# A decoder layer on one core: constants loaded in five groups, their splits placed in the engines' orders, and two semaphores for the pair moves

## The reference

```
kv_c = rms_norm(x @ W_kv) * g_kv ; q_c = x @ W_q                      # latents, 64 and 128 wide
k = [kv_c @ W_kdec | rope(x @ W_krope)] ; q = [q_c @ W_qdec | rope(q_c @ W_qrope)]
x = layernorm(x + softmax(causal(q k^T / sqrt(48))) (kv_c @ W_vdec) @ W_o)   # 16 heads
x = layernorm(x + softmax(x ctx^T / 4) ctx @ W^T + b)                         # 16 heads of 16
x = layernorm(x + sum over the top 2 of 8 experts of w_e * (gelu(x @ W1_e + b1_e) @ W2_e + b2_e))
```

## Time and profile before

| what | time |
|---|---|
| median of three runs | 777.57 us (777.42 to 779.69) |
| the profiled execution | 772.65 us |
| its span, from first to last instruction | 770.8 us |
| TensorE busy in the span | 630.1 us (82%) |
| mean granted clock of TensorE | 0.932 of 2.4 GHz |

### The profile page before, as it was taken

The page is one execution under the profiler, slowest core; times in us unless marked ns, Lnnn a source line. Parts: engine busy times, 40 slices in busy tenths (PEclk is TensorE's granted clock), DMA queues, the critical chain, the costliest instruction groups (busy, mean ns, idle before and its releaser), DMA issues.

```text
span 770.8 us, 22764 instructions
## 1 busy us (share of the span) xinstructions
PE 630.1 (82%) x8056; PEld 453.7 (59%) x8057; DVE 519.7 (67%) x1113; ACT 380.2 (49%) x791; POOL 320.6 (42%) x276
## 2 busy tenths in 40 slices
...
GB/s 237 58 148 124 206 63 119 40 104 26 98 70 14 112 42 73 69 26 114 71 97 137 56 82 74 64 28 43 41 41 44 52 41 41 48 47 41 43 32 213
DMA packets 39799, 59.34 MB, mean 77 GB/s; under 512 B 6736, under 2 KB 27472, under 8 KB 39600
## 3 DMA queue, kind: packets, MB, share of 16 engines
...
...
## 4 chain that ended last, share of the span: by engine, by line
PE 44%; DVE 11%; ACT 4%; DMA 3%; issue 3%; POOL 1%; ACTq 0%; DVEq 0%; POOLq 0%
PE bank L1562 7%; PE bank L1184 4%; PE bank L1564 4%; DVE mxc L946 3%; PE bank L1210 3%; PE bank L1552 3%; ACT probs L702 2%; PE max_scores L1552 2%; PE bank L1554 2%; DMA x_sb<-x_rows,slot_row 2%; PE max_scores L1554 2%; PE max_scores L1553 2%; PE bank L1553 2%; PE exp_scores L1538 2%; PE exp_scores L1249 2%
## 5 line engine op out<-in xcount | busy, mean ns | idle before, releaser
L702 ACT ACTIVATE probs<-exp_scores 128x768 f32<-128x768 f32 (+1 forms) x128 | 117.5, 918 | 111.7 <-PE exp_scores L1241 50.4
L606 POOL DMA_INDIRECT acc_rows<-x_res,slot_row x39 | 65.3, 1674 | 122.1 <-DVE x_res L1102 119.1
L1562 PE MATMUL bank<-w_sb,wp 128*128 x312 | 110.0, 380 | 2.0 <-DVE wp L1089 2.0
L946 DVE TENSOR_REDUCE mxc<-max_scores 128x4 f32<-128x1024 f32 x64 | 78.1, 1221 | 31.6 <-PE max_scores L1255 31.3
L1564 PE MATMUL bank<-w_sb,wp 128*128 x312 | 85.1, 273 | 0.0
L911 DVE TENSOR_REDUCE mx<-max_scores 128x6 f32<-128x768 f32 x64 | 60.9, 952 | 25.6 <-PE max_scores L1223 25.6
L1087 DVE CAST wp<-probs 128x512 f16<-128x512 f32 x78 | 33.6, 431 | 64.5 <-ACT probs L765 64.5
L765 ACT ACTIVATE probs<-bank,b_sb 128x128 f32<-128x128 f32 x152 | 43.5, 370 | 65.2 <-PE bank L1554 65.2
L765 ACT ACTIVATE probs<-max_scores,b_sb 128x128 f32<-128x128 f32 x160 | 45.6, 369 | 59.6 <-PE max_scores L1554 59.6
L1184 PE MATMUL bank<-probs,w_sb 128*32 128x256 f32 x768 | 58.6, 410 | 6.8 <-ACT probs L702 6.0
L1552 PE MATMUL max_scores<-xT,w_sb 128*128 128x128 f16 x320 | 60.5, 222 | 1.2 <-DVE xT L1081 1.2
...
## 6 DMA issues: line engine op xcount, KB each, us to landing
w_sb<-w_sb SPq DMA_DIRECT2D x192, 64.0 KB, 2.1
wstage<-in_w_exp SPq DMA_DIRECT2D x16, 512.0 KB, 4.0
w_sb<-in_w_exp SPq DMA_DIRECT2D x8, 512.0 KB, 4.0
wp<-in_w_exp SPq DMA_DIRECT2D x8, 512.0 KB, 4.2
...
```

Source lines behind the costliest of these rows:

```text
L606: nc.gpsimd.indirect_dma_start(out=acc_rows[:, :], out_offset=bass.IndirectOffsetOnAxis(ap=slot_row[:, n:n + 1], axis=0), in_=yb[n % 2], i ...
L702: nc.scalar.activation(probs[:, 2 * (k % 2):2 * (k % 2) + 2, 0:cols], ps_e[:, :, 0:cols], ACT.Exp, scale=(SELF_SCALE, CROSS_SCALE)[a]).the ...
L946: nc.vector.tensor_reduce(mxc[:, 2 * k:2 * k + 2, :], ps_m[:, :, :].rearrange("p h (a k) -> p h a k", a=2), axis=AX.X, op=ALU.max).then_in ...
L1562: mm(o[:, 0:2 * D], ah[:, u, f, :], weights(e, at, 2 * D), start=(f == 0), stop=(f == FC - 1), skip_group_check=True)
```

## The change

It does five things.

- The constants are five groups (`rl0` to `rl4`), each with a semaphore of its own, and are units of SyncE's order: `rl0` = w_kv and w_q, `rl1` = the rotated weights, `rl2` = the content weights and the values' weight, `rl3` = g_kv and the table, `rl4` = masks, wo, xb, wx, wg, bg, b1, followed by the stores of zero rows, for which SyncE no longer waits (`z_st`; ScalarE waits for it ahead of the first `sv`, GpSimd ahead of the gathers).
- The splits of projection weights are units: `ph0` to `ph2` on ScalarE, `pl0` to `pl2` on VectorE; the six copies of identity and masks are `mk`. TensorE waits at the first unit that needs each one.
- The raw weights lie elsewhere in the buffer, in an order that fits the groups.
- The moves of content raise `c_mv[k]`, the moves of rotated rows `r_mv[k]`, so casts and copies wait only for the moves that read what they overwrite.
- `cb` and `cw` use PSUM bank 3 and `cn` uses bank 0, where all three used bank 1. All five tables are new.

```diff
+    "rl": "load_constants", "ph": "projections_high", "pl": "projections_low", "mk": "masks",
 TENSOR_ORDER = """
-la.0 kt.0 qk0.0 qk1.0 qk2.0 qk3.0 va.0 la.1 ct0.0 ct1.0 kt.1 qk0.1 qk1.1 sm0.0 qk2.1 qk3.1 sm1.0 sm2.0 sm3.0 ct0.1
+la.0 kt.0 qk0.0 qk1.0 qk2.0 qk3.0 va.0 ct0.0 la.1 ct1.0 kt.1 qk0.1 sm0.0 ct0.1 qk1.1 sm1.0 qk2.1 sm2.0 qk3.1 sm3.0
...
 SYNC_ORDER = """
-x.0 w0.0 w1.0 c.0 w2.0 x.1 x.2 mc0.0 mc1.0 mc2.0 mv0.0 w3.0 mv1.0 x.3 mc3.0 mv2.0 mc4.0 mv3.0 mc5.0 mc6.0 w0.1 mv4.0
+w0.0 rl0.0 rl1.0 x.0 w1.0 rl2.0 rl3.0 x.1 w2.0 rl4.0 c.0 x.2 mv0.0 mv1.0 mc0.0 mc1.0 mc2.0 mc3.0 mv2.0 mc4.0 mc5.0
...
-        ps_max = [ps_x[i] for i in (2, 1)]
+        ps_max = [ps_x[i] for i in (2, 0)]
...
-        ps_back = [ps_x[i] for i in (0, 1)]
-        ps_out = [ps_x[i] for i in (0, 1)]
+        ps_back = [ps_x[i] for i in (0, 3)]
+        ps_out = [ps_x[i] for i in (0, 3)]
...
+                elif u == "load_constants":
+                    for dst, src in const_loads[k]:
+                        sp.dma_start(dst, src).then_inc((r_ld + [t_ld, c_ld])[k], 16)
+                    if k == 4:
+                        sp.wait_ge(c_ms, 1)
+                        sp.dma_start(x2_rows[TOK:ROWS, :], oP[0][:, 0, :]).then_inc(z_st, 16)
+                        sp.dma_start(acc_rows[TOK:ROWS, :], oP[0][:, 0, :]).then_inc(z_st, 16)
...
-            act_e.wait_ge(r_ld, 16 * N_RAW)
-            for at, end in W_RAW:
...
-            act_e.wait_ge(c_ld, 16 * N_LOADS)
             act_e.wait_ge(c_ms, 1)
-            act_e.wait_ge(pw_lo, 3)
-            act_e.wait_ge(x2_st, 32)
...
+                if u == "projections_high":
+                    act_e.wait_ge(r_ld[k], 16 * len(const_loads[k]))
+                    for at, end, rows in W_RAW[k]:
+                        last = nc.scalar.activation(wph[0:rows, at:end], raw(at, end - at, rows), ACT.Copy, scale=W_SCALE)
+                    last.then_inc(pw_hi, 1)
...
-            pe.wait_ge(c_ld, 16 * N_LOADS)
-            pe.wait_ge(c_bf, 1)
-            pe.wait_ge(pw_lo, 3)
...
                 if u == "latents":
                     bank1_free()
+                    once(pw_lo, 1)
...
                 elif u == "self_max":
+                    once(c_bf, 1)
                     maxima_free()
                     once(a_xc, at["stack"])
-                    pe.wait_ge(r_mv[k], b * 48 + 48)
+                    pe.wait_ge(r_mv[k], b * 32 + 32)
+                    pe.wait_ge(c_mv[k], b * 16 + 16)
```

More of the change, by code:

```diff
@@ L99 @@
-se4.3 cm5.2 se5.3 cm6.2 qk3.5 sv2.3 cm7.2 se6.3 sm0.4 se7.3 cn.2 sm1.4 sv3.3 ce0.2 x2.1 sm2.4 ce1.2 lg.1 sm3.4 ce2.2
-cv0.2 so.3 va.4 sm4.4 ce3.2 kt.5 sb.3 sm5.4 ce4.2 cv1.2 ct0.5 ct1.5 la.6 ce5.2 sw.3 sm6.4 cv2.2 ce6.2 sm7.4 ce7.2
-qk0.6 qk1.6 sn.4 st0.3 st1.3 cv3.2 se0.4 st2.3 st3.3 se1.4 co.2 cm0.3 sv0.4 se2.4 cm1.3 cb.2 se3.4 cm2.3 cw.2 cm3.3
-se4.4 sv1.4 cm4.3 qk2.6 se5.4 cm5.3 qk3.6 se6.4 x2.2 cm6.3 sv2.4 lg.2 cm7.3 se7.4 sm0.5 cn.3 sv3.4 sm1.5 ce0.3 va.5
-sm2.5 kt.6 ce1.3 so.4 sm3.5 cv0.3 sb.4 ce2.3 sm4.5 sw.4 ce3.3 sm5.5 la.7 cv1.3 ce4.3 sm6.5 ct0.6 ct1.6 ce5.3 sm7.5
@@ L114 @@
-gs1.5 cw.7 gs2.5 gs3.5 x2.7 gs4.5 lg.7 gs5.5 gr.7 gs0.7 gs1.7
+la.0 kt.0 qk0.0 qk1.0 qk2.0 qk3.0 va.0 ct0.0 la.1 ct1.0 kt.1 qk0.1 sm0.0 ct0.1 qk1.1 sm1.0 qk2.1 sm2.0 qk3.1 sm3.0
+ct1.1 la.2 sm4.0 sm5.0 sm6.0 sm7.0 qk0.2 sn.0 se0.0 qk1.2 se1.0 qk2.2 sv0.0 se2.0 qk3.2 se3.0 sm0.1 se4.0 sm1.1 sv1.0
+sm2.1 se5.0 kt.2 sm3.1 sv2.0 se6.0 sm4.1 se7.0 sm5.1 va.1 sv3.0 sm6.1 so.0 sm7.1 la.3 sb.0 ct0.2 sw.0 sn.1 ct1.2 se0.1
+se1.1 qk0.3 sv0.1 se2.1 qk1.3 st0.0 st1.0 qk2.3 st2.0 st3.0 se3.1 va.2 cm0.0 qk3.3 sv1.1 cm1.0 se4.1 kt.3 cm2.0 se5.1
@@ new lines @@
+cm3.0 sv2.1 cm4.0 se6.1 cm5.0 se7.1 cm6.0 sv3.1 cm7.0 so.1 sm0.2 cn.0 ct0.3 ce0.0 sm1.2 sb.1 ce1.0 ct1.3 sm2.2 cv0.0
+sm3.2 ce2.0 la.4 sm4.2 sw.1 ce3.0 sm5.2 qk0.4 cv1.0 ce4.0 sm6.2 qk1.4 ce5.0 qk2.4 sm7.2 ce6.0 cv2.0 st0.1 ce7.0 sn.2
+cm0.1 cv3.0 cm1.1 se0.2 co.0 st1.1 se1.2 st2.1 st3.1 se2.2 sv0.2 cm2.1 qk3.4 se3.2 cm3.1 cb.0 sv1.2 cm4.1 se4.2 cw.0
+cm5.1 se5.2 cm6.1 se6.2 sv2.2 cm7.1 va.3 se7.2 sm0.3 cn.1 kt.4 sv3.2 ce0.1 sm1.3 ce1.1 so.2 sm2.3 ce2.1 cv0.1 sb.2
+x2.0 sm3.3 ct0.4 sw.2 ce3.1 la.5 sm4.3 ce4.1 cv1.1 lg.0 sm5.3 ce5.1 ct1.4 sm6.3 ce6.1 sm7.3 cv2.1 st0.2 st1.2 sn.3
@@ new lines @@
+ce7.1 qk0.5 st2.2 cv3.1 se0.3 cm0.2 qk1.5 qk2.5 st3.2 se1.3 co.1 cm1.2 se2.3 sv0.3 cm2.2 se3.3 cm3.2 cb.1 sv1.3 se4.3
+cm4.2 cw.1 cm5.2 se5.3 cm6.2 se6.3 sv2.3 cm7.2 qk3.5 se7.3 sm0.4 cn.2 sv3.3 ce0.2 sm1.4 so.3 x2.1 ce1.2 sm2.4 lg.1
+cv0.2 sm3.4 ce2.2 sb.3 kt.5 sm4.4 ce3.2 va.4 sm5.4 cv1.2 sm6.4 ce4.2 ct0.5 la.6 sm7.4 ct1.5 ce5.2 sw.3 ce6.2 cv2.2
+qk0.6 ce7.2 qk1.6 sn.4 cv3.2 se0.4 st0.3 st1.3 se1.4 st2.3 st3.3 co.2 sv0.4 cm0.3 se2.4 cm1.3 cb.2 se3.4 cm2.3 cw.2
+cm3.3 sv1.4 se4.4 cm4.3 qk2.6 se5.4 cm5.3 qk3.6 se6.4 cm6.3 sv2.4 x2.2 cm7.3 se7.4 lg.2 cn.3 sm0.5 sv3.4 ce0.3 sm1.5
```

285 lines of the change are left out of this document (145 added, 140 removed).

## The result

The changed kernel takes 757.29 us (median of 4 runs, 755.5 to 758.69), beside 777.5 us for the kernel before on the same chip. The ratio is 0.9745 (0.970 to 0.979): 2.5% faster, 20 us, where 9.8 were forecast. The profiled execution took 757.2 us, against 772.65 before. The traces therefore account for 15.5 us of the 20: the profiled execution of before was faster than all four timed beside the changed kernel (773.36 to 779.69).

What follows compares the result with a forecast made beforehand. TensorE, working 82% of the span, and a 19.78 us start without matmuls were taken as the bounds. -9.7 + 0.4 (first latents) - 2.5 + 2.0 = -9.8 us, median 777.57 to 767.8; range 759 to 776.

Steps and rivals of the forecast that it cites:

- Banks and new orders: Between 60 and 480 us: same units in a slightly different sequence, work and dependences stay; taken as 0.
- two semaphores: Casts and copies no longer wait for moves of the other kind; SyncE's longest waits are for scores; 0 (-1 to 0).
- The bounds: Between 60 and 480 us: all 29.5 us of idle time gone, or one more 2.3 us wait per batch, +18.
- the price of a bad bank: Longest wait for a bank's maxima, 2.3 us, taken as one more wait in each of eight batches, +18.
- the new orders add to the gain: Rival, steady state: a fifth of TensorE's idle time goes (6 us), giving 762 us; chance 0.2.
- The start: Prologue: x lands at 8.0 us, first matmul at 10.1 instead of 19.78; -9.7 us (bounds -10.0 and -7.9).
- absorbed: Rival: the earlier start's gain is lost because a later release is late anyway; 775 to 779 us; chance 0.07.
- Group 4 and the masks: Batch 0: last constants landed by about 20 us, mask copies 0.9 us of VectorE ahead of first `sm`; cost 0.
- The cover: Batch 0: what was to hide 0.9 us of mask copies on VectorE; cost 0, or 0.9 us if it went.
- Moves and scores of batch 0: Batch 0, first rotation to `sm7.0`: rotated moves of pairs 0 and 1 go first; -2.5 us (-3.6 at most, or 0).
- The gate's last stretch: End of the gate: tile table now ahead of the one-hot pairs, delaying the 16 scatter matmuls; +2.0 us (0 to 3.5).
- The lower clock: Rival, batch 0: the earlier, sparser start runs wholly at 1.2 GHz, adding 4 us, giving 772; chance 0.15.

Runs made afterwards that it cites:

- all but the start: The changed kernel with the prologue of the kernel before put back, all constants loaded ahead of the tables and waited for: 763.65 us, ratio 0.985.
- the start alone: The kernel before with only the new prologue; orders otherwise, banks and the one semaphore for a pair's moves as before: 771.21 us, ratio 0.995.

## Why the prediction was wrong

*The direction was right, the size was not, and the larger part of the gain came from what I had put at 0.* Of the forecast -9.8, the start was -9.3 and the new orders -0.5 (moves -2.5, gate +2.0). Measured, the orders with their banks and semaphores gave -11.6, and the start, on top of them, -6.4 (-8 by the ratios). By the prediction's own steps:

- **Banks and new orders, 0, and two semaphores, 0: the step that failed.** The bounds (-29.5 to +18) held the truth, the choice did not. That the units stay the same said nothing on whether their waits do. Between 100 us and the end of the gate the time fell from 402.9 to 388.2 us; 6.3 of these 14.7 us are less busy time of TensorE (338.4 to 332.1, with 22 of 4743 matmuls fewer in the stretch and less time at the lower clock), the rest is idle time. The row I took as the price of a bad bank, 2.3 us for `negm`, was a wait that one moved unit took away; it was worth 4.5 us with the clock behind it. The rival "the new orders add to the gain" (762, 0.2) named the right place with too small a size: it priced idle time alone.
- **The semaphores by themselves.** I looked at what SyncE waits for, but it was ScalarE that waited for moves (7.5 us in the kernel before), and of its waits the prediction has not a word. On the old orders 0 was right even so. On the new ones merging them costs 12 us, of which the one wait on the content cast costs 7.
- **The start, -9.7.** Mis-sized: -8.3 at the first matmul (11.52). The pace assumed for the loads was too fast for x, which came sixth. (The bytes up to the table add up to 2961 KB, not 2968, which changes nothing.) That the start is handed on held in part: of about 8.5 us, 4.3 were left at `se0.0` and 6.3 at the gate's end on the new orders, 3.6 and 1.1 on the old ones. I had asked what the first matmul waits for, and not which lines the next 80 us hang on. The rival "absorbed" (0.07) describes the start on the old orders. That `sw.0` of the changed kernel stands where it stood before is a coincidence: 4.8 us earlier by the start, 4.6 later by the orders.
- **Group 4 and the masks, 0.** The cover was not there: 3.3 us of VectorE instead of 0.9, since the casts that I had read ran while GpSimd was idle. Moved ahead, the unit gave back 2.0 us at `se0.0`.
- **Moves and scores of batch 0, -2.5.** The sign was right for the orders: from the first rotation to `sm7.0` it is 30.9 us before and 29.8 with all but the start, 35.9 with the start alone and 33.75 in the changed kernel. The start, which I had taken to shift this stretch as it stands, lengthens it by 4 to 5 us.
- **The gate's last stretch, +2.0.** Measured 0: from `cw.7` to the end of the gate 29.8 us in both kernels. The scatter matmuls do start later behind `cw.7` (21.7 us instead of 20.5), but the 16 take 5.9 us instead of 6.6, and what follows them 0.5 less, as forecast.
- **The lower clock.** This rival (0.15) was half right. Worked out from the windows' clocks, TensorE has the lower clock for about 27 us of the first 100, instead of about 20, in the rival's direction. From 100 us to the end of the gate it is about 34 us instead of 49, which it did not see; over the execution the clock rose from 0.932 to 0.938.

What stays open: how much of the gain is each bank's by itself (the kernels for it moved units as well, but for the outputs' bank); why the start is kept on the new orders and lost on the old ones; and which places of the new orders, besides the one at 212 us, give the rest of the 16.5 us behind `sw.2`.
